# Cross attention on one core: moving the small per-column tiles ahead of the weights and cutting a filler tile, so that weights and data tiles start at the same place past 1024 bytes

## Chip, cores and metric

One Trainium2 chip, one NeuronCore of it. The metric is the device time of one execution in microseconds (us), the median of the runs shown. The kernel before takes 1264.02 us, median of 3 runs (1263.61 to 1264.63).

## What is computed

64 batches, each with 256 rows of x (512 wide) and 256 rows of a context (384 wide). In float32:

```python
text_p  = x @ W_text + b_text          # 64 x 256 x 512
audio_p = ctx @ W_audio + b_audio
Q = layer_norm(text_p, g1, beta1)
K = layer_norm(audio_p, g2, beta2)
alpha = softmax(Q @ K.T / sqrt(512))
H = (alpha @ audio_p) @ W_out + b_out
out = layer_norm(H + x, g_out, beta_out)
```

## The kernel before

The work goes in N = 32 steps, each of two batches (512 rows, four tiles t of 128). Every float32 operand of a product is split in two parts of the type float32r, a "hi" and a "lo" part, and every product is three matmuls: hi x hi, hi x lo, lo x hi. W_audio @ W_out is folded once at the start (the tiles `wao_hi`, `wao_lo`), so that the output product runs on probabilities times context.

What TensorE does in a step, in the order written out by hand in `products` (lines 493 to 515) and `scores`:

- `project_k` (L312 to L319, its matmuls at L302 to L304 by the helper `product`): 36 matmuls of 512 columns. The stationary operand, loaded by LDWEIGHTS, is a 128x128 block of `wa_hi`/`wa_lo`; the moving one is a row of `cT_hi`/`cT_lo`.
- `project_q` (L365 to L379, matmuls at L374, L377, L378): 48 of 512 columns, stationary `wt_hi`/`wt_lo`, moving `xT_hi`/`xT_lo`. After the first matmul of one group stands `mean_squares` (L384), one matmul of 512 columns with stationary `mean_of` and moving `sq_parts`.
- `probs_context` of the step before: 36 matmuls of 256 columns, stationary `c_hi`/`c_lo`, moving `pT_hi`/`pT_lo`, which are both data tiles.
- `output_part` (L425 to L434, matmuls at L430 to L432): 36 of 512 columns, stationary `pcT_hi`/`pcT_lo` (data tiles), moving `wao_hi`/`wao_lo` (weights). A second `mean_squares` stands among them.
- `scores` (L393 to L401): 48 of 256 columns, stationary `qT_hi`/`qT_lo`, moving `kT_hi`/`kT_lo`, all data tiles.

That is 122 matmuls of 512 columns and 84 of 256 in a step. ScalarE (ACT) makes the hi parts, squares, exponentials and part of the layer norms; VectorE (DVE) the lo parts, sums and normalizations; GpSimd (POOL) `c_lo`, some sums, the additions of `betao_row` (L1278) and two accumulating DMAs (L1255, L1268); the SP queue loads and stores. Only TensorE's order and the SBUF addresses matter for the change.

**Addresses.** The function `sb` (L34) takes SBUF in the order in which the tiles are named, each tile's bytes per partition rounded up to 32. `ident`, the first tile, starts 128 bytes past a multiple of 1024. Then come `ident` 512, `neg_half` 32, `neg_one` 32, `mean_of` 512, `eps` 32, so the six weight tiles (L49 to L51) start 224 past a multiple of 1024. All weight tiles and the three rows tiles `bao_row`, `go_row`, `betao_row` are multiples of 1024 long, so each of them starts at 224. Behind them stand the small tiles (L55 to L59: `cols` 96, `bac_col`, `btc_col`, `wa_mean`, `wt_mean`, `b_sum`, `b_mean` 32 each, 288 in all) and `b_shift` (L61), 96 bytes that no instruction uses. So the data tiles, `xT_in` to `pcT_lo` (L63 to L80), all multiples of 1024 long, start at 224 + 288 + 96 = 608 past a multiple of 1024. `mean_of` starts at 704.

Of the kernel before, what the change touches and what calls it, by code (L numbers as in the profile page):

```python
# [14 lines left out]
P = 128  # L15
# [3 lines left out]
def cross_attention_kernel(nc, x_rows, xT, c_rows, cT, columns, w_text, w_audio, w_out, b_out,  # L19
# [9 lines left out]
    DT, CT, HT = D // P, DC // P, H // P  # L29
# [3 lines left out]
    with ExitStack() as stack:  # L33
        def sb(name, shape, dt=F32):  # L34
            return stack.enter_context(nc.sbuf_tensor(name, shape, dt))
# [10 lines left out]
        mean_of = sb("mean_of", [P, P], F32R)  # L46
        eps = sb("eps", [P, 1])

        wt_hi, wt_lo = sb("wt_hi", [P, DT, H], F32R), sb("wt_lo", [P, DT, H], F32R)  # L49
        wa_hi, wa_lo = sb("wa_hi", [P, CT, H], F32R), sb("wa_lo", [P, CT, H], F32R)  # L50
        wao_hi, wao_lo = sb("wao_hi", [P, CT, H], F32R), sb("wao_lo", [P, CT, H], F32R)  # L51

        bao_row = sb("bao_row", [P, H])
        go_row, betao_row = sb("go_row", [P, H]), sb("betao_row", [P, H])
        cols = sb("cols", [P, 6, HT])  # L55
        ba_col, bt_col, g1_col, beta1_col, g2_col, beta2_col = (cols[:, n, :] for n in range(6))
        bac_col, btc_col = sb("bac_col", [P, HT]), sb("btc_col", [P, HT])
        wa_mean, wt_mean = sb("wa_mean", [P, CT]), sb("wt_mean", [P, DT])
        b_sum, b_mean = sb("b_sum", [P, 2]), sb("b_mean", [P, 2])  # L59

        b_shift = sb("b_shift", [P, 24])  # L61

        xT_in, cT_in = sb("xT_in", [P, DT, T * P]), sb("cT_in", [P, CT, T * P])  # L63
        c_kept = sb("c_kept", [P, T, DC])
# [1325 lines left out]
```

How the kernel before makes its waits and increments, by code:

```python
        def wait(eng, semaphore, value):  # L164
            if not isinstance(value, int) or value > 0:
                eng.wait_ge(semaphore, value)
# [1 line left out]
        def wait_apart(eng, semaphore, value):  # L169
            if not isinstance(value, int) or value > 0:
                eng.wait_ge(semaphore, value)
                eng.sem_inc(passed, 1)
# [16 lines left out]
        @block.sync  # L191
# [47 lines left out]
            def step(i, odd, first=False, last=False):  # L239
                if first:
                    wait_apart(sp, cT_split, CT)
                    load_cT(1)
                    load_rows()
                    load_c(0)
                    sp.wait_ge(x01_split, DT)
                elif isinstance(i, int) and i == 1:
                    sp.wait_ge(x01_split, 2 * DT)
                elif not last:
                    wait_apart(sp, xT_split, 16 * i - 16)
                if last:
                    sp.wait_ge(xT_split, 16 * (N - 2))
                    sp.dma_start(last_rows[:], x_rows[N - 1]).then_inc(x_last, 16)
                else:
                    load_xT(i + 1)
                if first:
                    sp.wait_ge(wao_done, CT)
                elif isinstance(i, int) and i == 1:
                    sp.wait_ge(bao_done, 1)
                if not isinstance(i, int) or i >= 2:
# [26 lines left out]
                sp.dma_start(out[N - 1, :, t, :], last_rows[:, t, :]).then_inc(stored[t], 16)  # L286
            for t in range(T):
                sp.wait_ge(stored[t], 16 * N)
```

## Time and profile before

| | before |
|---|---|
| median of 3 runs | 1264.02 us |
| the profiled execution: its time | 1264.63 us |
| its span, first to last instruction | 1262.8 us |
| granted TensorE clock, mean | 0.998 |
| PE busy | 1252.0 us (99%) |
| PEld (weight loads, beside PE) | 1067.9 us (85%) |
| DVE / ACT / POOL busy | 1079.8 / 1054.0 / 548.6 us |

A busy PE is modelled: consecutive matmuls overlap, so the mean duration of one (395 ns for 512 columns) is longer than the distance between two starts. The distance of starts is what adds up to the time.

### The profile page before, as it was taken

To read this page: it belongs to the slowest core of one execution; us is meant where nothing else is said; L and a number is where in the kernel's file an instruction comes from. 1 tells how busy PE (TensorE), PEld (TensorE's weight loads), DVE (VectorE), ACT (ScalarE), POOL (GpSimd) and SP (SyncE) were. 2 spreads that over 40 slices of the span, in tenths; PEclk is the share of its full clock that TensorE was granted. 3 is DMA by queue.
4 is the path that set the end of the run, shared out by engine and by line. 5 is a ranking of instruction groups with operands and counts; after the bars stand their busy time and mean duration, and the time that the engine had idled before them with its cause. 6 is when DMAs were issued, how large, how long until landed. Compare 5 with 4: busy or idle time off the path is not lost.

```text
span 1262.8 us, 22599 instructions
## 1 busy us (share of the span) xinstructions
PE 1252.0 (99%) x6662; PEld 1067.9 (85%) x6662; DVE 1079.8 (86%) x1735; ACT 1054.0 (83%) x1791; POOL 548.6 (43%) x545
## 2 busy tenths in 40 slices
PE   9999999999999999999999999999999999999997
PEld 7688888888888888888888888888888888888886
DVE  6788888898888888888988888988888888889888
ACT  7788888888888888888888888988888888888884
POOL 1132455433554434554435544335544345543356
PEclk9999999999999999999999999999999999999999
DMA  7356886776876767866668767678667688667693
GB/s 259 113 146 172 237 232 178 194 184 208 241 217 176 198 181 232 236 199 174 188 202 243 225 168 201 185 219 241 208 174 192 191 240 230 188 185 186 210 234 108
DMA packets 96645, 252.49 MB, mean 200 GB/s; under 512 B 9456, under 2 KB 25328, under 8 KB 88688
## 3 DMA queue, kind: packets, MB, share of 16 engines
q1 hardware_dynamic: 75408, 187.22, 42.2%
q0 software_dynamic: 21216, 65.02, 28.6%
q8 instruction: 10, 0.16, 0.0%
q14 instruction: 11, 0.09, 0.0%
HBM read 137.38 MB, written 49.81 MB: 148 GB/s over the span
## 4 chain that ended last, share of the span: by engine, by line
PE 95%; DVE 2%; ACT 2%; issue 1%; DMA 1%; SPq 0%; ACTq 0%; DVEq 0%
PE wide L374 9%; PE wide L377 9%; PE wide L378 9%; PE score L302 7%; PE score L303 7%; PE score L304 7%; PE wide L304 7%; PE wide L302 7%; PE wide L303 7%; PE wide L432 7%; PE wide L430 7%; PE wide L431 7%; PE turn L303 1%; PE turn L302 1%; PE turn L304 1%; PE turn L384 1%
## 5 line engine op out<-in xcount | busy, mean ns | idle before, releaser
L1278 POOL TENSOR_TENSOR y_rows<-y_rows,betao_row 128x512 f32<-128x512 f32 x120 | 166.6, 1388 | 338.8 <-ACT y_rows L652 226.0
L374 PE MATMUL wide<-xT_hi,wt_hi 128*128 128x512 f32 x496 | 195.8, 395 | 0.3 <-DVE xT_lo L863 0.3
L377 PE MATMUL wide<-xT_lo,wt_hi 128*128 128x512 f32 x496 | 195.8, 395 | 0.0
L378 PE MATMUL wide<-xT_hi,wt_lo 128*128 128x512 f32 x496 | 195.8, 395 | 0.0
L611 ACT ACTIVATE squares<-wide,bac_col 128x512 f32<-128x512 f32 x128 | 88.4, 690 | 77.1 <-PE wide L304 77.0
L304 PE MATMUL wide<-cT_hi,wa_lo 128*128 128x512 f32 x372 | 146.8, 395 | 0.0
L302 PE MATMUL wide<-cT_hi,wa_hi 128*128 128x512 f32 x372 | 146.8, 395 | 0.0
L432 PE MATMUL wide<-wao_hi,pcT_lo 128*128 128x512 f32 x372 | 146.7, 394 | 0.0
L430 PE MATMUL wide<-wao_hi,pcT_hi 128*128 128x512 f32 x372 | 146.7, 394 | 0.0
L303 PE MATMUL wide<-cT_lo,wa_hi 128*128 128x512 f32 x372 | 146.6, 394 | 0.0
L431 PE MATMUL wide<-wao_lo,pcT_hi 128*128 128x512 f32 x372 | 146.5, 394 | 0.0
L302 PE MATMUL score<-kT_hi,qT_hi 128*128 128x256 f32 x512 | 145.3, 284 | 0.7 <-DVE qT_lo L939 0.7
L304 PE MATMUL score<-kT_hi,qT_lo 128*128 128x256 f32 x512 | 144.7, 283 | 0.0
L303 PE MATMUL score<-kT_lo,qT_hi 128*128 128x256 f32 x512 | 144.7, 283 | 0.0
L1261 POOL TENSOR_TENSOR c_lo<-c_kept,c_hi 128x384 fp32r<-128x384 f32 x128 | 126.9, 1015 | 34.1 <-ACT c_hi L585 34.1
L1255 POOL DMA_DIRECT2D xT_lo<-xT_in x30 | 26.7, 889 | 216.0 <-ACT xT_lo L580 216.0
L643 ACT ACTIVATE qT_hi<-q_cols,cols 128x512 fp32r<-128x512 f32 x128 | 90.8, 726 | 28.6 <-DVE q_cols L933 26.0
L374 PEld LDWEIGHTS wide<-xT_hi,wt_hi 128*128 128x128 f32 x496 | 93.3, 188 | 22.8 <-issue 0.7
L378 PEld LDWEIGHTS wide<-xT_hi,wt_lo 128*128 128x128 f32 x496 | 93.3, 188 | 21.9
L377 PEld LDWEIGHTS wide<-xT_lo,wt_hi 128*128 128x128 f32 x496 | 93.2, 188 | 20.6
L939 DVE SCALAR_TENSOR_TENSOR qT_lo<-q_cols,cols,qT_hi 128x512 fp32r<-128x512 f32 x128 | 102.4, 800 | 8.5
L302 PEld LDWEIGHTS score<-kT_hi,qT_hi 128*128 128x128 f32 x512 | 97.9, 191 | 2.9 <-DVE qT_lo L939 1.3
(172 smaller groups left out, 3555.4 us busy)
## 6 DMA issues: line engine op xcount, KB each, us to landing
xT_in<-in_xT SPq DMA_DIRECT2D x31, 1024.0 KB, 8.6
y_rows<-in_x_rows SPq DMA_DIRECT2D x124, 256.0 KB, 4.1
y_rows<-bao_row POOLq DMA_DIRECT2D x31, 1024.0 KB, 9.4
out<-y_rows SPq DMA_DIRECT2D x124, 256.0 KB, 3.3
xT_lo<-xT_in POOLq DMA_DIRECT2D x30, 1024.0 KB, 8.9
c_kept<-in_c_rows SPq DMA_DIRECT2D x32, 768.0 KB, 6.8
cT_in<-in_cT SPq DMA_DIRECT2D x31, 768.0 KB, 8.8
p_out<-probs SPq DMA_DIRECT2D x31, 512.0 KB, 4.7
```

The source lines that it names most:

```text
L302: nc.tensor.matmul(to, a_hi, b_hi, start=(m == 0), stop=False)
L303: nc.tensor.matmul(to, a_hi, b_lo, start=False, stop=False)
L304: done = nc.tensor.matmul(to, a_lo, b_hi, start=False, stop=(m == n - 1))
L374: nc.tensor.matmul(wide[h][:], wt_hi[:, d, cols], xT_hi[:, d, :], start=(d == 0), stop=False)
L377: nc.tensor.matmul(wide[h][:], wt_hi[:, d, cols], xT_lo[:, d, :], start=False, stop=False)
L378: done = nc.tensor.matmul(wide[h][:], wt_lo[:, d, cols], xT_hi[:, d, :], start=False, stop=(d == DT - 1))
L430: nc.tensor.matmul(wide[t][:], hi, wao_hi[:, d, :], start=(d == 0), stop=False)
L431: nc.tensor.matmul(wide[t][:], hi, wao_lo[:, d, :], start=False, stop=False)
L432: done = nc.tensor.matmul(wide[t][:], lo, wao_hi[:, d, :], start=False, stop=(d == CT - 1))
L939: nc.vector.scalar_tensor_tensor(out=lo[:, h, :], in0=cols[:, h, :], scalar=shift[:, h:h + 1], in1=hi[:, h, :].bitcast(F32), op0=ALU.add, ...
L1261: nc.gpsimd.tensor_tensor(c_lo[:, t, :], c_kept[:, t, :], c_hi[:, t, :].bitcast(F32), ALU.subtract).then_inc(c_split, 1)
L1278: nc.gpsimd.tensor_tensor(rows, rows, betao_row[:], ALU.add).then_inc(y_ready, 1)
```

## The change

The seven small tiles and `b_shift` move in front of the weights, and `b_shift` shrinks from 24 to 8 columns (96 to 32 bytes). 288 + 32 = 320 bytes now stand ahead of the weights, which start at 224 + 320 = 544; the data tiles lie 64 bytes lower, at 608 - 64 = 544. No instruction, wait, queue or size changes.

```diff
         eps = sb("eps", [P, 1])
 
-        wt_hi, wt_lo = sb("wt_hi", [P, DT, H], F32R), sb("wt_lo", [P, DT, H], F32R)
-        wa_hi, wa_lo = sb("wa_hi", [P, CT, H], F32R), sb("wa_lo", [P, CT, H], F32R)
-        wao_hi, wao_lo = sb("wao_hi", [P, CT, H], F32R), sb("wao_lo", [P, CT, H], F32R)
-
-        bao_row = sb("bao_row", [P, H])
-        go_row, betao_row = sb("go_row", [P, H]), sb("betao_row", [P, H])
         cols = sb("cols", [P, 6, HT])
         ba_col, bt_col, g1_col, beta1_col, g2_col, beta2_col = (cols[:, n, :] for n in range(6))
         bac_col, btc_col = sb("bac_col", [P, HT]), sb("btc_col", [P, HT])
         wa_mean, wt_mean = sb("wa_mean", [P, CT]), sb("wt_mean", [P, DT])
         b_sum, b_mean = sb("b_sum", [P, 2]), sb("b_mean", [P, 2])
 
-        b_shift = sb("b_shift", [P, 24])
+        b_shift = sb("b_shift", [P, 8])
+
+        wt_hi, wt_lo = sb("wt_hi", [P, DT, H], F32R), sb("wt_lo", [P, DT, H], F32R)
+        wa_hi, wa_lo = sb("wa_hi", [P, CT, H], F32R), sb("wa_lo", [P, CT, H], F32R)
+        wao_hi, wao_lo = sb("wao_hi", [P, CT, H], F32R), sb("wao_lo", [P, CT, H], F32R)
+
+        bao_row = sb("bao_row", [P, H])
+        go_row, betao_row = sb("go_row", [P, H]), sb("betao_row", [P, H])
```

## Rows read from the trace of the kernel before

**Rows 1.** Busy time by stretch: start, the repeated steps, end. Columns are named.

```profile
core 0: us, PE busy (x) PEld busy (x) DVE busy (x) ACT busy (x) POOL busy (x), PEclk, DMA share, GB/s
0.00:48.20 48.20, 45.70 (x196) 32.83 (x197) 36.33 (x64) 38.54 (x68) 5.58 (x14) 1.00 0.50 173
48.20:1208.00 1159.80, 1159.54 (x6209) 995.50 (x6209) 998.32 (x1595) 981.40 (x1654) 513.88 (x503) 1.00 0.72 203
```

**Rows 2.** Waits between 100 and 1200 us: waiter, cause, total us, times, longest.

```profile
POOL y_rows L1278 <- ACT y_rows L652: 222.4, 29, 9.0
...
PEld turn L384 <- DVE sq_parts L863: 0.3, 1, 0.3
```

**Rows 3.** Timeline of PE: the first matmul of three steps. Start us, length, operation.

```profile
548.41 0.39 PE L302 MATMUL wide<-cT_hi,wa_hi 128*128 128x512 f32 x1
```

```profile
586.81 0.39 PE L302 MATMUL wide<-cT_hi,wa_hi 128*128 128x512 f32 x1
```

```profile
1048.01 0.39 PE L302 MATMUL wide<-cT_hi,wa_hi 128*128 128x512 f32 x1
```

**Rows 4.** Timeline of PE: inside one step, 512-column projections, then the change to context.

```profile
600.05 0.39 PE L378 MATMUL wide<-xT_hi,wt_lo 128*128 128x512 f32 x1
...
606.34 0.39 PE L378 MATMUL wide<-xT_hi,wt_lo 128*128 128x512 f32 x1
606.57 0.28 PE L302 MATMUL score<-pT_hi,c_hi 128*128 128x256 f32 x1
```

**Rows 5.** Timeline of PE around the second `mean_squares` of that step.

```profile
611.86 0.39 PE L431 MATMUL wide<-wao_lo,pcT_hi 128*128 128x512 f32 x1
612.09 0.39 PE L432 MATMUL wide<-wao_hi,pcT_lo 128*128 128x512 f32 x1
612.32 0.40 PE L384 MATMUL turn<-sq_parts,mean_of 128*128 128x512 f32 x1
612.55 0.39 PE L430 MATMUL wide<-wao_hi,pcT_hi 128*128 128x512 f32 x1
612.78 0.39 PE L431 MATMUL wide<-wao_lo,pcT_hi 128*128 128x512 f32 x1
```

**Rows 6.** Timeline of PE in `scores`: first and last of 40 matmuls, then the next step.

```profile
620.34 0.28 PE L303 MATMUL score<-kT_lo,qT_hi 128*128 128x256 f32 x1
```

```profile
625.02 0.28 PE L303 MATMUL score<-kT_lo,qT_hi 128*128 128x256 f32 x1
625.14 0.28 PE L304 MATMUL score<-kT_hi,qT_lo 128*128 128x256 f32 x1
625.26 0.39 PE L302 MATMUL wide<-cT_hi,wa_hi 128*128 128x512 f32 x1
```

**Rows 7.** Groups of weight loads by operands: count, busy us, mean ns of one, idle before.

```profile
L302 PEld LDWEIGHTS score<-kT_hi,qT_hi 128*128 128x128 f32 x512 | 97.9, 191 | 2.9 <-DVE qT_lo L939 1.3 <-issue 0.2
...
L374 PEld LDWEIGHTS wide<-xT_hi,wt_hi 128*128 128x128 f32 x496 | 93.3, 188 | 22.8 <-issue 0.7
...
L430 PEld LDWEIGHTS wide<-wao_hi,pcT_hi 128*128 128x128 f32 x372 | 70.1, 188 | 14.8
```

**Rows 8.** Groups on POOL and DVE whose operands lie at unlike and like places, same columns.

```profile
L933 DVE SCALAR_TENSOR_TENSOR k_cols<-k_cols,cols,turn 128x512 f32<-128x512 f32 x128 | 87.2, 743 | 4.8 <-ACT turn L634 3.8
...
L1025 DVE SCALAR_TENSOR_TENSOR y_rows<-y_rows,y_mv,go_row 128x512 f32<-128x512 f32 x90 | 64.9, 748 | 1.0
...
L1243 POOL TENSOR_TENSOR squares<-squares 128x512 f32<-128x512 f32 x32 | 41.6, 1299 | 51.6 <-ACT squares L611 51.6
...
L1276 POOL TENSOR_TENSOR y_rows<-y_rows,go_row 128x512 f32<-128x512 f32 x30 | 38.6, 1286 | 0.0
```

**Rows 9.** Timeline of DVE and the source view of L384 in that step: the tightest margin.

```profile
611.19 0.69 DVE L863 TENSOR_TENSOR sq_parts<-sq_half,sq_parts 64x512 fp32r<-64x512 f32 x1
```

```profile
L384 PEld LDWEIGHTS turn<-sq_parts,mean_of x2: 187/188/188, 599.4 to 612.1; 128*128 128x128 f32 x2
```

**Rows 10.** Chain that ended last, start us and length: the one DMA at the start.

```profile
4.48 6.71 DMA xT_in<-in_xT
```

More of the change, by code:

```diff
@@ L47, in cross_attention_kernel @@
         eps = sb("eps", [P, 1])
+        cols = sb("cols", [P, 6, HT])
+        ba_col, bt_col, g1_col, beta1_col, g2_col, beta2_col = (cols[:, n, :] for n in range(6))
+        bac_col, btc_col = sb("bac_col", [P, HT]), sb("btc_col", [P, HT])
+        wa_mean, wt_mean = sb("wa_mean", [P, CT]), sb("wt_mean", [P, DT])
+        b_sum, b_mean = sb("b_sum", [P, 2]), sb("b_mean", [P, 2])
+        b_shift = sb("b_shift", [P, 8])
         wt_hi, wt_lo = sb("wt_hi", [P, DT, H], F32R), sb("wt_lo", [P, DT, H], F32R)
@@ L54, in cross_attention_kernel @@
         go_row, betao_row = sb("go_row", [P, H]), sb("betao_row", [P, H])
[L55 to L59, printed above, removed]
-        b_shift = sb("b_shift", [P, 24])
         xT_in, cT_in = sb("xT_in", [P, DT, T * P]), sb("cT_in", [P, CT, T * P])
```

## The prediction

> **What bounds the kernel now.** I read the busy times by stretch first, then the waits, then TensorE's own timeline. Between 48.2 and 1208.0 us PE is busy for 1159.54 of 1159.80 us at a granted clock of 1.00 [rows 1], the 2.4 GHz level. The waits say the same: in the middle of the run POOL waits for hundreds of microseconds in total, while for TensorE one wait of 0.3 us is left [rows 2]. So nothing holds TensorE up in the repeated steps. DVE with 998.32 us and ACT with 981.40 us of that stretch have 14% and 15% to spare [rows 1].
>
> The time is therefore TensorE's pace. Two neighbouring steps start 586.81 - 548.41 = 38.40 us apart, and twelve steps take 1048.01 - 586.81 = 461.20 us, 38.43 each [rows 3]. Inside a step, 27 matmuls of 512 columns lie between 600.05 and 606.34, 233 ns from start to start [rows 4]; 39 of 256 columns lie between 620.34 and 625.02, 120 ns each [rows 6]. 122 x 0.233 + 84 x 0.120 = 28.4 + 10.1 = 38.5 us: the paces account for the step. Only what changes one of these two paces, or makes TensorE wait, can change the time by more than a little.
>
> **The change, part by part.** The instruction stream is the same; only addresses differ. Seven terms.
>
> 1. *Weights against data, 512 columns.* In the projections the stationary operand (weights, at 224) and the moving one (data, at 608) lie 384 bytes apart, counted past 1024; in the output product it is the other way round. After the change both lie at 544, so they are 0 or 512 apart (blocks of weights are 512 bytes long). Does this pairing have a price? The trace already holds 512-column intervals with like places. While `sq_parts` (608) streams from 612.32, the weights loaded for the next matmul are `pcT_hi` (608): 0.23 us to 612.55, as for its neighbours, 0.23 each [rows 5]. While `xT_hi` (608) streams from 606.34, the weights loaded are `c_hi` (608): 0.23 us to 606.57 [rows 4]. Both recur in every repeated step, some 30 times each. The display has steps of 10 ns, so a single such interval excludes only 10 ns or more.
> 2. *The same pairing, 256 columns.* In `scores` both operands are data tiles, 0 or 512 apart, at 120 ns. The one interval per step in which the load behind such a matmul comes from the weights at 224 is 625.14 to 625.26, again 0.12 us [rows 6]. So at 256 columns like and unlike places give the same pace.
> 3. *The loads themselves.* A load takes 188 ns where it comes from `wt_hi` at 224 beside data at 608, 188 where it comes from `pcT_hi` at 608 beside weights at 224, and 191 in `scores` with both at 608 [rows 7]. Like places may lengthen a load by 3 ns. The load runs beside the matmul before it and ends 233 - 188 = 45 ns before the next one is due, so 3 ns would be covered; without that cover it is 3 ns per matmul.
> 4. *The place itself.* All weights move from 224 to 544, all data from 608 to 544. Counted past 64 bytes all stay at 32; counted past 128 they move from 96 to 32. No matmul of size in the trace has a moving operand at 32 past 128. The nearest row with another place is the load of `mean_of` (704, which is 64 past 128): 187 or 188 ns [rows 9]. I take zero, and keep the bounds of terms 1 and 3 for it.
> 5. *DVE, ACT and POOL.* The rows tiles `go_row` and `betao_row` come to like places with `y_rows`. Like and unlike places cost the same now: 1299 ns on POOL for two operands in `squares`, 1286 with `go_row`; on DVE 748 with `go_row`, 743 where the other operand is in PSUM [rows 8]. Zero. Their cover is large in any case but at one place: `sq_parts` is finished at 611.19 + 0.69 = 611.88 and the load for L384 starts at 612.1 [rows 9], 0.2 us later. An operation of 0.69 us there would have to take 0.2 us more, a third of itself, before TensorE waited; past that, its lateness would be paid once a step, 31 times.
> 6. *Start and end.* 48.2 us before the first repeated step and 54.8 us after 1208 us are not all PE; DVE and ACT operations and one DMA of 6.71 us [rows 10] are in the chain. A per cent on the 100 us would be 1 us. I take zero, with 0.5 us either way, mostly for that DMA.
> 7. *Filler.* Nobody reads or writes `b_shift`; its shrinking acts only through term 4.
>
> Sum: 0, give or take 0.5 us. Against the profiled execution, 1264.63 us with a span of 1262.8 and 1.8 around it, the forecast is 1264.6; that execution was the slowest of three, 0.6 us above their median, so for the median I say 1264.0. A measurement of this kernel tells about 0.2% (2.5 us) from no change. With some 3720 matmuls of 512 columns (31 x 120) this is 0.7 ns for each: the question is whether the pace of a 512-column matmul moves by as little as 0.3%.
>
> **Rivals.**
>
> *A conflict goes away (faster).* The second 256 columns of a matmul cost 233 - 120 = 113 ns [rows 4, 6], where 256 columns at 2.4 GHz are 106.7. About 6 ns of each 512-column matmul are thus unexplained, and they appear exactly where weights meet data at unlike places. If they are a conflict between the load and the stream, like places could remove them: 3720 x 6 ns = 22 us, 1242 us. Against it: intervals with like places at 512 columns are 0.23 too [rows 4, 5], and the 6 ns would have to vanish below what 10 ns steps show. The full excess over the bare stream is 233 - 213 = 20 ns, 74 us, the far end.
>
> The Trainium skill, page "TensorE: Matmul & The Clock Gate", section "Back-to-back issue gap", puts the isolated gap at the columns over 2.4 GHz plus about 2.5 ns, 216 ns at 512 columns. The trace has 233, so by that rule there is something for a placement to win, and the sum would be 3720 x 17 ns = 63 us less, 1201 us. The rule is one for matmuls without a load between them, and no run here shows such a stream; the forecast doesn't use it.
>
> *A conflict appears (slower).* Load and stream now start at the same place past 1024 in every projection and output matmul and collide as they begin. Price: the 3 ns by which loads are longer at like places [rows 7], if they reach the pace: 3720 x 3 = 11 us, 1275 us; at 10 ns, the most that the display could hide in term 1, 37 us, 1301 us. It decides from 0.7 ns per matmul on. For it: the 191. Against it: the 45 ns of cover, and `scores`, whose pace of 120 ns is the same with the weights' load behind it.
>
> *The change does not do what it says.* 224 + 288 + 32 and 608 - 64 are both 544, and no tile between has a length that is no multiple of 1024. I give this nothing.
>
> **Chances.** No change 0.75: like places are already in the trace, on TensorE, DVE and POOL, with no price. Faster 0.13, slower 0.12: both need an effect that the 10 ns steps hide, or one of the untried place 32 past 128, which could go either way, and small effects of 3 to 6 us are in them as well as the priced ones. The no-change case alone spans 1262.5 to 1265.6; I reach to 1259.0 and 1268.5 to take in a shift of about 1 ns per wide matmul (3.7 us) and the spread of the runs.
>
> **What would show it.** Right: steps of 38.40 to 38.45 us, 27 wide matmuls in 6.29 us, loads of 188 and 191 ns, one DVE wait of PE at most in the middle, busy PE of the stretch unchanged. The faster rival shows as 0.227 us from wide start to wide start and steps of about 37.8 us with `scores` still at 120 ns; the slower one as loads above 188 in the groups at L302 to L304 `wide`, L374 to L378 and L430 to L432, and steps over 38.8 us. If steps keep their length and the time moves, it came from start or end, and term 6 is wrong. If PE waits for DVE at L384, term 5 is.

## The result and the profile after

The changed kernel takes 1248.41 us (median of 4 runs, 1248.05 to 1248.9) against 1264.01 us before: a ratio of 0.9876, interval 0.9864 to 0.9888. That is 15.6 us faster, where no change was forecast. The profiled execution took 1248.9 us with a span of 1247.1, 15.7 us less than the 1262.8 of before.

Line numbers of `kernel.py` are one higher than before: L302 to L304 are now L303 to L305, L374/L377/L378 are L375/L378/L379, L384 is L385, L430 to L432 are L431 to L433.

Busy time by stretch, the same columns as in [rows 1]:

```profile
core 0: us, PE busy (x) PEld busy (x) DVE busy (x) ACT busy (x) POOL busy (x), PEclk, DMA share, GB/s
0.00:48.60 48.60, 45.19 (x197) 32.35 (x197) 36.34 (x64) 38.56 (x68) 5.64 (x15) 1.00 0.50 171
48.60:1191.70 1143.10, 1142.79 (x6206) 992.57 (x6205) 1001.67 (x1595) 977.98 (x1654) 514.98 (x502) 1.00 0.73 205
```

PE is still all of the middle, at the same granted clock of 1.00. The start is as long as it was (48.6 against 48.2 us), and DVE, ACT and POOL did the same work in the same time to 0.4%. What shrank is the middle. The timeline of PE at the first matmul of two steps, twelve steps apart, as in [rows 3]:

```profile
579.76 0.40 PE L303 MATMUL wide<-cT_hi,wa_hi 128*128 128x512 f32 x1
```

```profile
1034.56 0.40 PE L303 MATMUL wide<-cT_hi,wa_hi 128*128 128x512 f32 x1
```

Twelve steps take 454.80 us, 37.90 each; they took 461.20, 38.43 each. 30 times 0.53 us is 15.9 us: the whole gain. Inside a step, 27 matmuls of `project_q`, as in [rows 4]:

```profile
592.76 0.39 PE L379 MATMUL wide<-xT_hi,wt_lo 128*128 128x512 f32 x1
```

```profile
598.88 0.39 PE L379 MATMUL wide<-xT_hi,wt_lo 128*128 128x512 f32 x1
```

6.12 us for 27 intervals is 226.7 ns, 544 periods of 2.4 GHz: 512 columns and 32 more. Before it was 6.29 us, 233 ns. The groups of the costliest matmuls (count, busy us, mean ns of one), all engine PE:

```profile
L375 PE MATMUL wide<-xT_hi,wt_hi 128*128 128x512 f32 x496 | 193.0, 389 | 0.3 <-DVE xT_lo L864 0.3
...
L303 PE MATMUL wide<-cT_hi,wa_hi 128*128 128x512 f32 x372 | 145.1, 390 | 0.0
...
L305 PE MATMUL score<-kT_hi,qT_lo 128*128 128x256 f32 x512 | 144.9, 283 | 0.0
```

The modelled mean of a 512-column matmul went from 395 to 389 ns; that of a 256-column one stayed at 283. This mean rises and falls with the interval to the next start (395 stands with 232 to 233 ns, 389 to 391 with 227 to 228), so it is a handy sign. Weight loads did not change:

```profile
L375 PEld LDWEIGHTS wide<-xT_hi,wt_hi 128*128 128x128 f32 x496 | 93.1, 188 | 20.0 <-issue 0.7
```

188 ns, as in [rows 7]: the duration of a load shows nothing of what follows.

One thing is new. The waits between 100 and 1180 us, weight loads only (waiter, cause, total us, times, longest):

```profile
PEld turn L385 <- DVE sq_parts L864: 6.2, 28, 0.4
```

Before, the list had one such wait of 0.3 us [rows 2]; now each step has one, 0.22 us on average. It shows in the timelines of DVE and of the weight loads around one `mean_squares`:

```profile
591.47 0.68 DVE L864 TENSOR_TENSOR sq_parts<-sq_half,sq_parts 64x512 fp32r<-64x512 f32 x1
```

```profile
591.80 0.19 PEld L375 LDWEIGHTS wide<-xT_hi,wt_hi 128*128 128x128 f32 x1
592.20 0.19 PEld L385 LDWEIGHTS turn<-sq_parts,mean_of 128*128 128x128 f32 x1 [0.21 <-DVE sq_parts L864]
592.31 0.19 PEld L378 LDWEIGHTS wide<-xT_lo,wt_hi 128*128 128x128 f32 x1
```

and in that of the matmuls:

```profile
592.02 0.39 PE L375 MATMUL wide<-xT_hi,wt_hi 128*128 128x512 f32 x1
592.25 0.45 PE L385 MATMUL turn<-sq_parts,mean_of 128*128 128x512 f32 x1
592.54 0.39 PE L378 MATMUL wide<-xT_lo,wt_hi 128*128 128x512 f32 x1
```

`sq_parts` is finished at 592.15, the load of `mean_of` was due at 592.03 and starts at 592.20, and the matmul after `mean_squares` starts 0.29 us behind it instead of 0.23. That costs TensorE 0.06 us a step.

The same place in the kernel before, which [rows 9] doesn't show (timelines of DVE and of the weight loads):

```profile
598.69 0.69 DVE L863 TENSOR_TENSOR sq_parts<-sq_half,sq_parts 64x512 fp32r<-64x512 f32 x1
```

```profile
599.12 0.19 PEld L374 LDWEIGHTS wide<-xT_hi,wt_hi 128*128 128x128 f32 x1
599.43 0.19 PEld L384 LDWEIGHTS turn<-sq_parts,mean_of 128*128 128x128 f32 x1
```

`sq_parts` was finished at 599.38, and the load, due at 599.12 + 0.23 = 599.35, started 0.05 us after that: in each step TensorE already met DVE at the first `mean_squares`, with a load that came 0.08 us late, and its matmuls were not held up by more than a few ns. The margin of 0.2 us in [rows 9] is that of the second `mean_squares`, and not the tightest. In the changed kernel both loads start 0.05 us behind `sq_parts`.

### The profile page after: what moved, and what is told of

The parts are those of the page before. It is cut to its first block, busy times and chain, and to the rows that moved or that the text cites. A ratio compares the mean times of both kernels' runs of the same rounds, so it can differ in the third digit from the quotient of the medians.

```text
span 1247.1 us, 22599 instructions
## 1 busy us (share of the span) xinstructions
PE 1235.1 (99%) x6662; PEld 1065.1 (85%) x6662; DVE 1083.9 (87%) x1735; ACT 1050.8 (84%) x1791; POOL 551.2 (44%) x545
## 4 chain that ended last, share of the span: by engine, by line
PE 93%; DVE 3%; ACT 2%; issue 1%; DMA 1%; SPq 0%; DVEq 0%; ACTq 0%
PE wide L375 9%; PE wide L379 9%; PE wide L378 9%; PE score L304 7%; PE score L303 7%; PE score L305 7%; PE wide L303 7%; PE wide L304 7%; PE wide L305 7%; PE wide L431 7%; PE wide L433 7%; PE wide L432 7%; PE turn L385 1%; PE turn L304 1%; PE turn L305 1%; PE turn L303 1%
## 5 line engine op out<-in xcount | busy, mean ns | idle before, releaser
L375 PE MATMUL wide<-xT_hi,wt_hi 128*128 128x512 f32 x496 | 193.0, 389 | 0.3 <-DVE xT_lo L864 0.3
L378 PE MATMUL wide<-xT_lo,wt_hi 128*128 128x512 f32 x496 | 193.0, 389 | 0.0
L379 PE MATMUL wide<-xT_hi,wt_lo 128*128 128x512 f32 x496 | 193.0, 389 | 0.0
L303 PE MATMUL score<-kT_hi,qT_hi 128*128 128x256 f32 x512 | 145.4, 284 | 0.8 <-DVE qT_lo L940 0.8
L431 PE MATMUL wide<-wao_hi,pcT_hi 128*128 128x512 f32 x372 | 145.4, 391 | 0.0
L433 PE MATMUL wide<-wao_hi,pcT_lo 128*128 128x512 f32 x372 | 145.2, 390 | 0.0
L303 PE MATMUL wide<-cT_hi,wa_hi 128*128 128x512 f32 x372 | 145.1, 390 | 0.0
L304 PE MATMUL wide<-cT_lo,wa_hi 128*128 128x512 f32 x372 | 145.1, 390 | 0.0
L305 PE MATMUL score<-kT_hi,qT_lo 128*128 128x256 f32 x512 | 144.9, 283 | 0.0
L304 PE MATMUL score<-kT_lo,qT_hi 128*128 128x256 f32 x512 | 144.9, 283 | 0.0
L305 PE MATMUL wide<-cT_hi,wa_lo 128*128 128x512 f32 x372 | 144.7, 389 | 0.0
L432 PE MATMUL wide<-wao_lo,pcT_hi 128*128 128x512 f32 x372 | 144.7, 389 | 0.0
L375 PEld LDWEIGHTS wide<-xT_hi,wt_hi 128*128 128x128 f32 x496 | 93.1, 188 | 20.0 <-issue 0.7
L379 PEld LDWEIGHTS wide<-xT_hi,wt_lo 128*128 128x128 f32 x496 | 93.1, 188 | 19.4
L378 PEld LDWEIGHTS wide<-xT_lo,wt_hi 128*128 128x128 f32 x496 | 93.2, 188 | 18.2
L303 PEld LDWEIGHTS score<-kT_hi,qT_hi 128*128 128x128 f32 x512 | 98.1, 192 | 2.9 <-DVE qT_lo L940 1.4
```

The source lines that it names most:

```text
L303: nc.tensor.matmul(to, a_hi, b_hi, start=(m == 0), stop=False)
L304: nc.tensor.matmul(to, a_hi, b_lo, start=False, stop=False)
L305: done = nc.tensor.matmul(to, a_lo, b_hi, start=False, stop=(m == n - 1))
L375: nc.tensor.matmul(wide[h][:], wt_hi[:, d, cols], xT_hi[:, d, :], start=(d == 0), stop=False)
L378: nc.tensor.matmul(wide[h][:], wt_hi[:, d, cols], xT_lo[:, d, :], start=False, stop=False)
L379: done = nc.tensor.matmul(wide[h][:], wt_lo[:, d, cols], xT_hi[:, d, :], start=False, stop=(d == DT - 1))
```

## The experiments

Two theories stood after the result. **Like places:** the load of the next weights and the stream of the present data disturb each other, depending on the distance between the two addresses. **The place itself:** what counts is where a tile starts past 128 bytes (96 before, 32 after). Each kernel below changes only the order of the small tiles and unused filler tiles, unless its diff says more. A distance is the place of the data tiles less that of the weight tiles, past 1024 bytes. Runs without an interval are one run, beside the kernel before on the same chip: one run of 1264.68 us for the first four (both at 608, distances 384, 320 and 64), one of 1265.35 for the second four (256, 192, 32, output product alone). Line numbers of these kernels are within two of those before. Where a mean interval in nanoseconds is given, it is taken from the start times of the matmuls of the repeated steps, for the projections those of `project_k`; the fences carry the modelled means that go with it.

**Both at 608.** The changed kernel with a filler of 96 bytes.

```diff
-        b_shift = sb("b_shift", [P, 8])
+        b_shift0 = sb("b_shift0", [P, 24])
```

> The layout of the change, with the filler at 96 bytes instead of 32: weights and data both at 608 past 1024, the place that the data had before. Theory 'like places' (what counts is the distance between weights and data): 512-column matmuls start 226 to 228 ns apart as in the changed kernel, time about 1248 us. Theory 'the place itself' (what counts is where a tile starts past 128 bytes: 96 costs, 32 does not): 232 to 233 ns as before, about 1264 us.

1249.22 us, as fast as the change, with data where they were before and all at 96 past 128. Projections 227.5 ns (as in the changed kernel, its first five intervals of a step included), output product 227.5 ns.

**Distance 384, all at 32 past 128.**

```diff
-        neg_half, neg_one = sb("neg_half", [P, T]), sb("neg_one", [P, 1])
+        neg_half = sb("neg_half", [P, T])
         mean_of = sb("mean_of", [P, P], F32R)
-        eps = sb("eps", [P, 1])
 ...
         go_row, betao_row = sb("go_row", [P, H]), sb("betao_row", [P, H])
+        neg_one = sb("neg_one", [P, 1])
+        eps = sb("eps", [P, 1])
 ...
-        b_shift = sb("b_shift", [P, 24])
+        b_shift0 = sb("b_shift0", [P, 8])
```

The weights then start at 160, the data at 544.

> Weights at 160, data at 544 past 1024: the distance of before (384), with every tile at 32 past 128 as in the changed kernel. 'Like places': 232 to 233 ns, about 1264 us. 'The place itself': 226 to 228 ns, about 1248 us.

1263.65 us, as slow as before, 232.4 ns and 232.2 ns. The place past 128 bytes is out: it was 96 for all in the fast kernel and is 32 for all in the slow one. One group of each of the two kernels, both at 608 first:

```profile
L300 PE MATMUL wide<-cT_hi,wa_hi 128*128 128x512 f32 x372 | 145.1, 390 | 0.0
```

```profile
L300 PE MATMUL wide<-cT_hi,wa_hi 128*128 128x512 f32 x372 | 146.8, 395 | 0.0
```

**Data alone, weights alone.** The layout of before with the filler at 32 bytes (weights 224, data 544, distance 320); and the changed kernel with 64 unused bytes ahead of the data (544 and 608, distance 64).

```diff
-        b_shift = sb("b_shift", [P, 24])
+        b_shift0 = sb("b_shift0", [P, 8])
```

```diff
         go_row, betao_row = sb("go_row", [P, H]), sb("betao_row", [P, H])
+        b_shift1 = sb("b_shift1", [P, 16])
         xT_in, cT_in = sb("xT_in", [P, DT, T * P]), sb("cT_in", [P, CT, T * P])
```

> Half of the change: the layout of before with only the filler shrunk to 32 bytes. Weights stay at 224 (96 past 128), data go to 544 (32 past 128), distance 320. 'The place itself', if the moving operand's place counts: projections at 226 to 228 ns, the output product (moving weights) at 232, about 1253 us. 'Like places': the distance is neither 0 nor 384, so slow unless only some distances conflict: 232 ns and 1264 us, or something between.

> The other half: weights at 544 as in the change, data at 608 as before, distance 64. 'The place itself' by the moving operand: projections at 232, the output product at 226 to 228, about 1260 us. 'Like places': at a distance of 64 either a slow pace (1264 us), or a fast one if a small distance is as good as none (1248 us).

1258.29 and 1257.98 us, in between, and the two are alike. In `project_k` both repeat one series of three intervals, 226, 229 and 232 ns (each to 1 ns), through all 36 matmuls; the output product is at 233.5 and 233.2 ns. In the groups of the first of the two:

```profile
L428 PE MATMUL wide<-wao_hi,pcT_hi 128*128 128x512 f32 x372 | 146.8, 395 | 0.0
...
L302 PE MATMUL wide<-cT_hi,wa_lo 128*128 128x512 f32 x372 | 146.6, 394 | 0.0
L301 PE MATMUL wide<-cT_lo,wa_hi 128*128 128x512 f32 x372 | 145.8, 392 | 0.0
...
L300 PE MATMUL wide<-cT_hi,wa_hi 128*128 128x512 f32 x372 | 144.3, 388 | 0.0
```

Two things follow. Distances 320 and 64 differ by 256 and do the same. And the same two places cost more when the weights are the moving operand and the data the stationary one (233) than the other way round (229), as in the output product, where moving less stationary is -64: the sign seems to count.

**Distance 256.** The changed kernel with `y_bn`, `y_mv`, `y_sc`, `neg_max` and `row_sum` (256 bytes) moved from the end to just ahead of the data.

```diff
         go_row, betao_row = sb("go_row", [P, H]), sb("betao_row", [P, H])
+        y_bn, y_mv = sb("y_bn", [P, T, 6]), sb("y_mv", [P, T, 2])
+        y_sc = sb("y_sc", [P, T, 3])
+        neg_max = sb("neg_max", [P, T])
+        row_sum = sb("row_sum", [P, T])
         xT_in, cT_in = sb("xT_in", [P, DT, T * P]), sb("cT_in", [P, CT, T * P])
```

> Weights at 544, data at 800 past 1024, distance 256. So far distance 64 and distance 320 gave the projections one and the same series of intervals (226, 229, 232 ns), which says that the distance counts past 256. By that, 256 is as good as 0: 226 to 228 ns, about 1248 us. If it counts past 512 or 1024, 256 is a distance like any other: 229 ns or more, 1256 to 1264 us.

1248.42 us, 227.5 and 226.9 ns: as good as 0. The distance counts past 256.

```profile
L301 PE MATMUL wide<-cT_hi,wa_hi 128*128 128x512 f32 x372 | 145.1, 390 | 0.0
...
L430 PE MATMUL wide<-wao_lo,pcT_hi 128*128 128x512 f32 x372 | 144.8, 389 | 0.0
```

**Distance 192.** Weights at 288, data at 480: 64 the other way round, past 256. `b_shift` of 64 bytes ahead of the weights, `y_bn`, `y_mv` and `y_sc` (192 bytes) between, the other small tiles behind the data.

> Weights at 288, data at 480, distance 192, which past 256 is the distance 64 the other way round. If the sign counts and places count past 256, the projections take what the output product took at distance 64 (233 ns), and the output product takes what the projections took (229 ns): 84 x 233 + 36 x 229 + 2 and the rest, about 1261 to 1263 us. If only the size of the distance counts, the two stay as they were, about 1258 us.

1263.68 us, just above the 1261 to 1263 expected if the sign counts; projections 233.4, output product 229.3 ns. The two groups have changed places, so it is the sign of the distance, not the product. One group of each:

```profile
L372 PE MATMUL wide<-xT_hi,wt_hi 128*128 128x512 f32 x496 | 196.1, 395 | 0.2 <-DVE xT_lo L861 0.2
...
L429 PE MATMUL wide<-wao_lo,pcT_hi 128*128 128x512 f32 x372 | 145.3, 391 | 0.0
```

**Distance 32.** The changed kernel with 32 unused bytes ahead of the data.

```diff
         go_row, betao_row = sb("go_row", [P, H]), sb("betao_row", [P, H])
+        b_shift1 = sb("b_shift1", [P, 8])
```

> Weights at 544, data at 576, distance 32, the smallest that the rounding of tiles allows. If a conflict needs the two reads in different blocks of 64 bytes or more, 32 is as good as 0: about 1248 us. If it grows with the distance from 0 (64: 229 and 233 ns), something between, about 1253 us, with the output product slower than the projections.

1266.79 us, the slowest of all, 1.4 us above its neighbour of before; 233.3 and 232.8 ns. Both expectations missed: the cost does not grow with the distance. The projections pay no more than at 192 (233.4); the kernel is slower than that one because its output product, whose distance is -32, pays in full too and doesn't fall to 229.

```profile
L376 PE MATMUL wide<-xT_lo,wt_hi 128*128 128x512 f32 x496 | 195.9, 395 | 0.0
L431 PE MATMUL wide<-wao_hi,pcT_lo 128*128 128x512 f32 x372 | 147.2, 396 | 0.0
```

**The output product alone.** The kernel before with `wao_hi` and `wao_lo` moved behind the filler, to 608. Projections stay at distance 384.

```diff
-        wao_hi, wao_lo = sb("wao_hi", [P, CT, H], F32R), sb("wao_lo", [P, CT, H], F32R)
 ...
-        b_shift = sb("b_shift", [P, 24])
+        b_shift0 = sb("b_shift0", [P, 24])
+        wao_hi, wao_lo = sb("wao_hi", [P, CT, H], F32R), sb("wao_lo", [P, CT, H], F32R)
```

> The kernel before with only wao_hi and wao_lo moved behind the small tiles, to 608, where the data are; projections keep the distance 384. If the gain belongs to each pair of operands, the output product alone goes from 232.2 to about 227.5 ns and the projections stay at 232.5: 36 x 31 x 4.7 ns = 5 us less than before, about 1259 us. If the gain needs the whole step in like places, or comes from anything other than these pairs (rows tiles with DVE and POOL, columns), it is 1264 us.

1258.67 us, 6.7 below its neighbour, where 5 had been expected. By the traces a step is 38.24 us for 38.43, 5.8 us in all; the rest is within the spread of single runs of the kernel before (1263.45 to 1265.35). Output product 227.6, projections 232.4:

```profile
L372 PE MATMUL wide<-xT_hi,wt_hi 128*128 128x512 f32 x496 | 195.6, 394 | 0.3 <-DVE xT_lo L861 0.3
...
L429 PE MATMUL wide<-wao_lo,pcT_hi 128*128 128x512 f32 x372 | 144.9, 389 | 0.0
```

The gain belongs to the pair of operands of each product. Past 1024 bytes only `wao_hi` and `wao_lo` changed their place (the rows tiles and small tiles lie 12288 bytes lower), and in a repeated step nobody but TensorE reads them, so neither other engines nor the DMAs are in it.

**Scores at unlike places.** The changed kernel with `qT_hi` and `qT_lo` moved behind `pcT_lo`, 128 unused bytes ahead of them.

```diff
-        qT_hi, qT_lo = sb("qT_hi", [P, HT, T * P], F32R), sb("qT_lo", [P, HT, T * P], F32R)
 ...
         pcT_hi, pcT_lo = sb("pcT_hi", [P, CT, T * P], F32R), sb("pcT_lo", [P, CT, T * P], F32R)
+        b_apart = sb("b_apart", [P, 32])
+        qT_hi, qT_lo = sb("qT_hi", [P, HT, T * P], F32R), sb("qT_lo", [P, HT, T * P], F32R)
```

> The changed kernel with qT_hi and qT_lo 128 bytes further on (672 past 1024, kT stays at 544): only the operands of the 256-column matmuls in scores come to unlike places. If matmuls of 256 columns are hit as those of 512, by 5.7 ns each or by half of it, the steps grow by 48 x 2.9 to 5.7 ns, 4 to 8.5 us in all: 1252.5 to 1257 us. If 256 columns leave it room, 120 ns stay and so does 1248.4 us.

1249.09 us, 15.7 below the kernel before on its chip (1264.79, median of 10), as much as the change gains. The intervals in `scores` are no longer all 120 but 118, 120, 122 in turn, with a mean of 120.1 against 119.8 ns: 0.3 ns, where 512 columns pay 5.7. Matmuls of 256 columns feel the distance and hardly pay for it.

One interval of 512 columns was changed as well, the last of the output product. Its own operands are still at like places; what is unlike is `qT_hi` (672), loaded while `wao_hi` (544) streams:

```profile
611.61 0.40 PE L434 MATMUL wide<-wao_hi,pcT_lo 128*128 128x512 f32 x1
611.84 0.29 PE L304 MATMUL score<-kT_hi,qT_hi 128*128 128x256 f32 x1
```

Over all steps it went from 226.8 to 232.7 ns. That speaks for the load of the next weights as the party that disturbs the stream, though the first matmul of `scores`, whose start ends the interval, has unlike operands of its own.

**`mean_of` at a like place.** Its distance of 160 was the last unlike one. It is moved behind the filler (`mean_of` at 32, weights and data at 544).

```diff
-        mean_of = sb("mean_of", [P, P], F32R)
 ...
-        b_shift = sb("b_shift", [P, 8])
+        b_shift0 = sb("b_shift0", [P, 8])
+        mean_of = sb("mean_of", [P, P], F32R)
```

> The changed kernel with mean_of too at a like place past 256 (at 32 past 1024, weights and data at 544). In the changed kernel the intervals are irregular for some six matmuls behind the second mean_squares and in the first six of a step (233, 236, 228 ...). If mean_of's distance of 160 starts them, those behind mean_squares go to 227 and the step is shorter by about 0.04 us, 1.2 us in all: 1247 us. If they come from the change of 256 to 512 columns, nothing moves: 1248.4 us.

1248.49 us, ratio to before 0.9878 (0.9862 to 0.9895): no gain over the change. The irregular intervals stayed, in the first five matmuls of a step and behind `mean_squares`. In the changed kernel, at the start of a step (timeline of PE):

```profile
580.23 0.39 PE L305 MATMUL wide<-cT_hi,wa_lo 128*128 128x512 f32 x1
580.45 0.40 PE L303 MATMUL wide<-cT_hi,wa_hi 128*128 128x512 f32 x1
580.69 0.39 PE L304 MATMUL wide<-cT_lo,wa_hi 128*128 128x512 f32 x1
580.92 0.39 PE L305 MATMUL wide<-cT_hi,wa_lo 128*128 128x512 f32 x1
```

The first five intervals take 580.92 - 579.76 = 1.16 us, 232 ns each; only then comes the even 227, although every pair of operands in them lies at like places. A change from 256 to 512 columns does not explain them by itself: the output product follows the context product, of 256 columns, and its first intervals in the same step are 228, 226 and 227.

**First `mean_squares` one matmul later**, on top of the last kernel:

```diff
-                    if d == mean_at:
-                        mean_squares(i, turn[0][:], k_sq_parts, k_var)
                     nc.tensor.matmul(wide[h][:], wt_hi[:, d, cols], xT_lo[:, d, :], start=False, stop=False)
+                    if d == mean_at:
+                        mean_squares(i, turn[0][:], k_sq_parts, k_var)
```

> The same, and the first mean_squares of a step stands one matmul later, behind the second product of its group. In the changed kernel the load of mean_of waits for sq_parts in each step and the interval behind mean_squares is 287 ns, 60 more than its neighbours. If that wait is the cause, 30 x 0.06 = 1.8 us go: about 1245.5 us with the run above at 1247. If the 60 ns belong to the pair of operands and not to the wait, nothing moves.

1250.32 us, ratio to before 0.9892 (0.9875 to 0.9909), 1.8 slower than the kernel it was made from. The 60 ns at the first `mean_squares` did go (227 ns there). But its result comes later and DVE's chain after it too: in one step of each kernel the second `sq_parts` is finished 25.01 us after the step's start, 24.83 in the kernel it was made from. So the second one now waits more. Timeline of PE:

```profile
605.35 0.39 PE L430 MATMUL wide<-wao_hi,pcT_lo 128*128 128x512 f32 x1
605.62 0.50 PE L382 MATMUL turn<-sq_parts,mean_of 128*128 128x512 f32 x1
605.96 0.40 PE L428 MATMUL wide<-wao_hi,pcT_hi 128*128 128x512 f32 x1
```

0.27 and 0.34 us where 0.227 is due: 0.15 us a step for 0.06 saved (some 0.01 of the 0.15 was there already). The waits of the loads between 100 and 1180 us say the same; in the kernel it was made from they were 28, with 6.1 us in total, all at the first `mean_squares`:

```profile
PEld turn L382 <- DVE sq_parts L861: 8.9, 30, 0.3
```

**Both later.** The second one too, behind the output matmuls of tile 2.

```diff
                 output_part(j, 1, 0)
-                mean_squares(i, turn[1][:], q_sq_parts, q_var)
                 for t in range(2, T):
                     pe.wait_ge(q_centred, HT * i + t + 1)
                     output_part(j, t, 0)
+                    if t == 2:
+                        mean_squares(i, turn[1][:], q_sq_parts, q_var)
```

> The kernel of the run before (mean_of at a like place, first mean_squares one matmul later) with the second mean_squares too moved, behind the output matmuls of tile 2, some 0.7 us later. There the second one cost 152 ns a step by waiting for sq_parts, more than the 60 ns that went at the first. If the wait is only a matter of when TensorE comes by, it goes: step 37.82 us, about 1246 us. If the sums behind it (reciprocal root, normalization, q parts) then come too late for the scores, the time is lost there instead, in the first matmuls of scores, and it stays at 1248 us or more.

1260.78 us, ratio to before 0.9969 (0.9957 to 0.998). Both waits at `mean_squares` are gone, and all intervals around them are an even 227: the irregular ones there came with the late load. The first five of a step stayed. The time is lost in `scores`, in each step: the ninth interval is 539 ns on average and the tenth 222 instead of 120, for the lo part of q. Waits of the loads between 100 and 1180 us:

```profile
PEld score L300 <- DVE qT_lo L938: 13.0, 28, 0.5
```

So the place of `mean_squares` in the changed kernel is the best of the three tried, and no kernel here beats the change.

## Why the prediction was wrong

*What bounds the kernel* was right: TensorE's pace, with no waits in the middle. *Terms 2, 6 and 7* held. 256 columns kept their 120 ns; the start is 0.4 and the end 0.6 us longer; the filler did nothing but shift. *Term 5* held in its prices: with `go_row` 1287 ns on POOL and 746 on DVE, for 1286 and 748. (One group on DVE did get longer, the additions of `squares` at L905, 753 ns for 689, but both at 608 and distance 256 have that too, 751 and 761, and distance 384 at 32 past 128 hasn't, so it goes with TensorE's pace and not with a place.) But by the prediction's own sign, PE waiting for DVE at L384, term 5 failed in its margin.

*Term 1 failed*, and with it the sum. It put the price of unlike places at zero, and at the distance of before they cost some 5.7 ns in each 512-column matmul. It read two single intervals with like places, 0.23 us each [rows 4, 5], as showing that the pairing has no price. The display's 10 ns steps were not what misled it: averaged over all steps of that trace, the two intervals are 231.8 and 232.8 ns, no faster than their neighbours' 232.5. An interval does not depend on its own pair alone. In the changed kernel five intervals of 232 ns on average pass at like places before the pace settles. In the kernel before, `project_k` repeats a series of seven, from 228 to 241 ns, while its operands come back in threes, so matmuls of the same tiles take different intervals. That a single like interval amid unlike ones takes the pace of its neighbours fits the two above, and the like interval at the end of `project_q` at distance 32 (233.3 beside 233.4); at distance 64 it is 233.2 beside 229.4, so the rule is not exact, and it is a reading and not tested. Only a stretch of many tells, and before the change no such stretch of 512 columns existed; `scores`, which is one, has 256 columns, and these hardly pay at the one other distance tried (118, 120, 122 at distance 128).

*Term 3*, the loads of 191 ns in `scores`, pointed the wrong way. Loads for 512-column matmuls take 188 ns in the fast and the slow kernel. Those of `scores` do get shorter at unlike places (188 to 190 ns for 192 in the changed kernel), but they are covered, as the term said. *Term 4*, the untried place 32 past 128, was a real gap in the evidence but an idle one: both at 608 was fast, distance 384 at 32 past 128 was slow.

*The faster rival* had the place, and the mechanism as far as it is shown: 6 ns in each 512-column matmul, a conflict of load and stream that like places remove. It was given 0.13. Its size was right per matmul (233 to 226.7 ns) and too large in the sum, 22 us for 15.6. Per step 120 x 5.7 = 0.68 us were to be had and 0.53 came. Of the 0.15 missing, 0.06 is the wait for `sq_parts`, 0.03 the first five matmuls, some 0.04 the ones around the second `mean_squares`, and 0.02 the context product (121.0 ns for 120.5). *Term 5* had asked about just this wait and missed it twice. It took the margin of the second `mean_squares`, 0.2 us, for the tightest, where the load of the first was already 0.08 us late in each step; and it asked what a slower DVE would do, and not what a faster TensorE would meet.

A finer reading of the two intervals of term 1 would have said the same. Still, that it excluded "only 10 ns or more" should have kept a 6 ns effect at more than 0.13: the evidence named against the rival was, by its own account, too coarse for it.

## What to carry over

Where TensorE's pace is the bound and weights change at every matmul, try the stationary and the moving tiles of each product at the same address past 256 bytes; a filler of 32 to 224 bytes, or another order of the small tiles, is all that it takes, and here, with float32r matmuls of 512 columns whose blocks and rows all start at multiples of 512 bytes within their tiles, it was worth 1.2%. Other types and widths were not tried. Test it by the average interval over a long stretch of one product: single intervals, load durations and the busy share show nothing. When TensorE gets faster, look at the margins of what it waits for, because the smallest of them comes up next; moving the waiting matmul by hand moved the loss and made it larger.

## What was not expected of the hardware

A 512-column float32r matmul with its own weight load takes 226.7 ns from start to start, once the pace has settled, where the distance of the operands past 256 bytes is 0, and by distance (moving less stationary): 233 at 32, 229 at 64, 232 at 128, 233 at 192 and at 224. The groups of loads for them average 187 to 189 ns in all kernels, and the clock granted in the repeated steps was 1.00. Counted in periods of 2.4 GHz, 226.7 ns is 512 + 32 and the 120 ns of 256 columns is 256 + 32: at like places the pace is the columns and 32 more, at unlike ones 5 to 16 more are added to 512 columns, and one to 256 (0.3 ns at distance 128, the only one measured).

The Trainium skill, page "SBUF — State Buffer", section "SBUF: two separate sides", says that TensorE never waits on anyone for SBUF, and gives its weight loads a second, independent read port. The waits of TensorE in these traces are for results of DVE and not for access, so no run here speaks against the first. But the pace depends on the addresses of its own two operands against each other, so the two reads don't look independent, and there the measurement decides: 5.7 ns in 232. The page "TensorE: Matmul & The Clock Gate", section "Back-to-back issue gap", has 216 ns for the isolated gap at 512 columns, and about 131 ns for each matmul of that size in a sustained stream of loads and matmuls. It names no type for them. The best that any kernel here reached with a load for each float32r matmul is 226.7, and the measurement decides.

Open stays why 256 bytes is the measure, why the sign of the distance counts at 64 (229 against 233) and not at 32 (233 both ways), and what makes the first five intervals of a step slow. That the load of the next weights is the other party is not shown outright: the pair's addresses are all that was varied, and the one interval before the moved `qT_hi` fits it, but no kernel ran a stream without loads. Distances of less than 32 bytes were not tried.
